# Performer and gated block on one core: the keys pass with its random features in four row tiles, one job order per engine, and the value parts kept twice

## The reference, cut to what matters

```python
q = jnp.einsum('bsd,dhk->bhsk', x, wq)
k = jnp.einsum('bsd,dhk->bhsk', x, wk)
v = jnp.einsum('bsd,dhk->bhsk', x, wv)

def _phi(u, omega):                       # omega: 128 x 32
    proj = jnp.einsum('bhsk,mk->bhsm', u, omega)
    sq = 0.5 * jnp.sum(u * u, axis=-1, keepdims=True)
    stab = jnp.max(proj, axis=-1, keepdims=True)
    return jnp.exp(proj - sq - stab) / jnp.sqrt(m) + 1e-06

pk = _phi(k * scale, omega)
kv = jnp.einsum('bhsm,bhsk->bhmk', pk, v)  # sum over the rows s
z = jnp.sum(pk, axis=2)
```

## Time and profile before

| | |
|---|---|
| median of three runs | 3862.85 us (3861.43 to 3863.89) |
| the profiled execution, its own time | 3863.65 us |
| its span, first to last instruction | 3861.9 us |
| mean granted clock of PE | 0.973 of full |
| keys pass | from 0 to about 1019 us of the span |
| groups in the keys pass | 32, one each 30.9 us in the middle |

### The profile page before, as it was taken

One profiled execution on the slowest core, in us unless ns is written; L12 is line 12 of the kernel. 1 busy time (PEld: TensorE's weight loads), 2 busy tenths in 40 slices (PEclk: granted clock), 3 DMA queues, 4 the chain that ended last, 5 costly groups with the idle time before them and its releaser, 6 DMA issues. The chain is left out here.

```text
span 3861.9 us, 70764 instructions
## 1 busy us (share of the span) xinstructions
PE 3656.8 (95%) x25330; PEld 3166.0 (82%) x25330; DVE 2275.3 (59%) x3627; ACT 1838.2 (48%) x3947; POOL 1379.4 (36%) x956
## 2 busy tenths in 40 slices
PE   7999999999599999999999976999999999999998
PEld 6777777777488888888888866888888998888987
DVE  6777777777567877878778853333333333333332
ACT  5666666666455655656556643332323323223322
POOL 3344444434334544445445441222222222222222
PEclk9999999999799999999999998999999999999999
DMA  3222222122223232223222323111111111111111
GB/s 107 85 79 75 85 81 81 71 87 82 101 83 100 85 100 92 92 85 100 87 92 91 105 79 123 44 49 50 53 43 43 43 43 43 43 43 43 43 43 49
DMA packets 155048, 282.63 MB, mean 73 GB/s; under 512 B 23568, under 2 KB 44560, under 8 KB 153872
## 3 DMA queue, kind: packets, MB, share of 16 engines
q1 hardware_dynamic: 154896, 280.42, 21.5%
HBM read 166.08 MB, written 114.29 MB: 73 GB/s over the span
## 5 line engine op out<-in xcount | busy, mean ns | idle before, releaser
L1480 DVE TENSOR_TENSOR ffn_hT_lo<-ffn_hid,ffn_hT_hi 128x512 fp32r<-128x512 f32 x256 | 334.6, 1336 | 491.0 <-ACT ffn_hT_hi L1456 491.0
L96 PE MATMUL ffn_hidden<-ffn_yT_hi,ffn_wa_hi 128*128 128x256 f32 x2048 | 573.7, 280 | 11.6 <-DVE ffn_yT_lo L1476 11.6
L96 PE MATMUL ffn_hidden<-ffn_yT_hi,ffn_wa_lo 128*128 128x256 f32 x2048 | 573.9, 280 | 0.0
L96 PE MATMUL ffn_hidden<-ffn_yT_lo,ffn_wa_hi 128*128 128x256 f32 x2048 | 572.9, 280 | 0.0
L1447 ACT ACTIVATE ffn_hid<-ffn_hidden,ffn_bias 128x256 f32<-128x256 f32 x512 | 213.2, 467 | 674.0 <-PE ffn_hidden L96 621.9
L96 PE MATMUL ffn_result<-ffn_wb_hi,ffn_hT_hi 128*128 128x512 f32 x1024 | 412.2, 403 | 7.5 <-DVE ffn_hT_lo L1480 7.4
L274 POOL TENSOR_TENSOR ffn_n_rstd<-ffn_n_base,ffn_n_power 128x2 f32<-128x2 f32 x32 | 22.4, 699 | 1080.3 <-DVE ffn_n_negmean L269 1080.3
L96 PE MATMUL ffn_result<-ffn_wb_hi,ffn_hT_lo 128*128 128x512 f32 x1024 | 404.5, 395 | 0.0
L96 PE MATMUL ffn_result<-ffn_wb_lo,ffn_hT_hi 128*128 128x512 f32 x1024 | 404.2, 395 | 0.0
L96 PEld LDWEIGHTS ffn_hidden<-ffn_yT_hi,ffn_wa_hi 128*128 128x128 f32 x2048 | 385.1, 188 | 20.6 <-DVE ffn_yT_lo L1476 11.9
L96 PEld LDWEIGHTS ffn_hidden<-ffn_yT_lo,ffn_wa_hi 128*128 128x128 f32 x2048 | 385.5, 188 | 8.9
(11 more groups left out here) (231 smaller groups left out, 10062.4 us busy)
## 6 DMA issues: line engine op xcount, KB each, us to landing
attend_uq<-u_d SPq DMA_DIRECT2D x33, 512.0 KB, 3.6
ffn_y_in<-y_d SPq DMA_DIRECT2D x33, 512.0 KB, 3.6
keys_xin<-in_L_attn_x_dram SPq DMA_DIRECT2D x32, 512.0 KB, 4.0
xn_d<-keys_xn SPq DMA_DIRECT2D x32, 512.0 KB, 2.8
xT_d<-keys_xT_whole SPq DMA_DIRECT2D x32, 512.0 KB, 2.9
u_d<-keys_uq SPq DMA_DIRECT2D x32, 512.0 KB, 2.8
attend_xTf<-xT_d SPq DMA_DIRECT2D x32, 512.0 KB, 5.0
r_d<-attend_gate SPq DMA_DIRECT2D x32, 512.0 KB, 2.8
```

Source lines behind the costliest of these rows:

```text
L96: last = pe.matmul(out, stationary[a], moving[b], start=start and n == 0, stop=stop and n == len(TERMS) - 1)
L1480: dve.tensor_tensor(hT[n % HB].lo[:, :, :], hid[n % 2][:, :, :], f32(hT[n % HB].hi[:, :, :]), ALU.subtract).then_inc(h_ready[n % HB], 1)
```

## The change

- **Features of a whole tile in four row tiles.** The matrix `bd` goes, and omega transposed (`omT`, 128 partitions that hold it four times below each other, 128 columns) takes its place. The job `proj` n is now for tile n with all its 16 heads: for each of four chunks and three terms, four matmuls, one for each head of the chunk, with 32 partitions (a row tile) by 128 columns, each into its own bank `feat[j]`. The four banks hold a whole tile, once. The second tile waits until the exponentials of the first have read them. `top` is then four reductions of 512 columns for a tile and one `below` of 16 columns. The eight banks are now two `dense`, four `feat`, one `turn` and one `kv`; before they were two each of `dense`, `turn`, `proj` and `kv`.
- **An order of jobs for each engine.** `BODY` becomes `PE_BODY`, `DVE_BODY`, `ACT_BODY`, `POOL_BODY` and `SP_BODY`. exp, hi, pk and z are jobs for one tile and one chunk (n = 4 t + c).
- **Buffers.** `v_parts` is kept twice, by the parity of the group. `e` and `pk` hold all four chunks of each tile. `kv_sum` has the whole bank, diagonal blocks and the rest, so that DVE adds 128 partitions by 512 in one operation for each chunk; the store picks the blocks that are wanted, in two DMAs. The stages for the weights lie in `e` and `z_sum`.
- **Loops.** The four groups of a sequence are written out, with a loop over sequences only.

```diff
-        BODY = [("whole", 0, 1), ("x", 0, 2), ("proj", 0, 0), ("top", 0, 0), ("hi", 0, 0), ("k", 0, 1),
-                ("top", 1, 0), ("pk", 0, 0), ("proj", 1, 0), ("hi", 1, 0), ("k", 1, 1), ("proj", 2, 0),
-                ("top", 2, 0), ("hi", 2, 0), ("pk", 1, 0), ("kv", 0, 0), ("stats", 0, 2), ("top", 3, 0), ("q", 0, 1),
-                ("norm", 0, 2), ("pk", 2, 0), ("kv", 1, 0), ("proj", 3, 0), ("hi", 3, 0), ("q", 1, 1), ("pk", 3, 0),
-                ("turn_k", 0, 1), ("turn_k", 1, 1), ("v", 0, 1), ("kv", 2, 0), ("kv", 3, 0), ("v_out", 0, 1),
-                ("v", 1, 1), ("v_out", 1, 1), ("turn_x", 0, 2), ("turn_x", 1, 2)]
+        PE_BODY = [("proj", 0, 0), ("k", 0, 1), ("k", 1, 1), ("q", 0, 1), ("proj", 1, 0), ("turn_k", 0, 1),
+                   ("q", 1, 1), ("v", 0, 1), ("turn_k", 1, 1), ("kv", 0, 0), ("v", 1, 1), ("kv", 1, 0), ("kv", 2, 0),
+                   ("turn_x", 0, 2), ("kv", 3, 0), ("turn_x", 1, 2)]
+        DVE_BODY = [("top", 0, 0), ("sq", 0, 1), ("pk", 0, 0), ("top", 1, 0), ("pk", 1, 0), ("turn_k", 0, 1),
+                    ("pk", 2, 0), ("pk", 3, 0), ("pk", 4, 0), ("stats", 0, 2), ("pk", 5, 0), ("kv", 0, 0),
+                    ("turn_k", 1, 1), ("pk", 6, 0), ("kv", 1, 0), ("pk", 7, 0), ("sq", 1, 1), ("kv", 2, 0),
+                    ("turn_x", 0, 2), ("v_out", 0, 1), ("kv", 3, 0), ("turn_x", 1, 2), ("v_out", 1, 1)]
+        ACT_BODY = [("k", 0, 1), ("exp", 0, 0), ("exp", 1, 0), ("exp", 2, 0), ("exp", 3, 0), ("hi", 0, 0),
+                    ("k", 1, 1), ("hi", 1, 0), ("q", 0, 1), ("hi", 2, 0), ("turn_k", 0, 1), ("hi", 3, 0),
+                    ("exp", 4, 0), ("hi", 4, 0), ("exp", 5, 0), ("q", 1, 1), ("hi", 5, 0), ("exp", 6, 0),
+                    ("turn_k", 1, 1), ("hi", 6, 0), ("exp", 7, 0), ("hi", 7, 0), ("norm", 0, 2), ("turn_x", 0, 2),
+                    ("v_out", 0, 1), ("turn_x", 1, 2), ("v_out", 1, 1)]
+        POOL_BODY = [("z", 0, 0), ("z", 1, 0), ("z", 2, 0), ("z", 3, 0), ("stats", 0, 2), ("z", 4, 0),
+                     ("whole", 0, 1), ("z", 5, 0), ("z", 6, 0), ("z", 7, 0)]
+        SP_BODY = [("x", 0, 2), ("whole", 0, 1), ("q", 1, 1), ("norm", 0, 2), ("sums", 0, 0)]
...
 # PE
                 if job == "proj":
-                    pe.wait_ge(turn[n // 2].free, 2 * g + 2)
-                    for t in range(TG):
-                        wait(pe, e_ready[t], NC * g + n)
-                        product(pe, proj[t].t[:, :], kT[:, n, t * P:(t + 1) * P], bd[:, :], start=True, stop=True)\
-                            .then_inc(proj[t].full, 1)
+                    pe.wait_ge(turn.free, 4 * g + 4)
+                    wait(pe, e_ready[1 - n], NC * g + NC if n == 1 else NC * g)
+                    for c in range(NC):
+                        for k, (x_, y_) in enumerate(TERMS):
+                            for j in range(HC):
+                                last = pe.matmul(feat[j].t[:, c * M:(c + 1) * M],
+                                                 kT[rows(j), c, n * P:(n + 1) * P][x_], omT[rows(j), :][y_],
+                                                 start=k == 0, stop=k == 2)
+                                if c == NC - 1 and k == 2:
+                                    last.then_inc(feat[j].full, 1)
                 if job == "kv":
-                    wait(pe, kv[n % 2].free, 2 * g + n // 2)
+                    wait(pe, kv.free, NC * g + n)
...
 # ACT
                 if job == "turn_x":
                     wait(act, xT_whole_ready, g)
-                    act.wait_ge(turn[n].full, 2 * g + 1)
+                    act.wait_ge(turn.full, 4 * g + n + 1)
...
                 if job == "v_out":
                     act.wait_ge(dense[n].full, 3 * g + 3)
-                    for m in range(2):
-                        wait(act, kv[m].full, 2 * g)
-                    act.activation(v_part[:, n, :, 0, :], by_head(dense[n].t), ACT.Copy).then_inc(v_hi, 1)
+                    wait(act, kv.full, NC * (g - 1))
+                    act.activation(v_part[i % 2][:, n, :, 0, :], by_head(dense[n].t), ACT.Copy).then_inc(v_hi, 1)
...
+                if job == "exp":
+                    t, c = n // NC, n % NC
+                    if c == 0:
+                        act.wait_ge(below_ready, TG * g + t + 1)
...
+                    wait(act, pk_ready[t], NC * (g - 1) + c + 1)
+                    wait(act, z_added[t], NC * (g - 1) + c + 1)
+                    for j in range(HC):
+                        h = c * HC + j
+                        last = act.activation(e[t][:, c, j * M:(j + 1) * M], feat[j].t[:, c * M:(c + 1) * M],
+                                              ACT.Exp, bias=below[:, t, h:h + 1])
+                    last.then_inc(e_ready[t], 1)
...
 # DVE
+                if job == "top":
+                    t = TG * g + n
+                    for j in range(HC):
+                        dve.wait_ge(feat[j].full, t + 1)
+                        dve.tensor_reduce(top[:, n, :, j:j + 1], feat[j].t[:, :].rearrange("p (c m) -> p c m", c=NC),
+                                          AX.X, ALU.max).then_inc(top_ready, 1)
+                    dve.wait_ge(sq_ready[n], g + 1)
+                    dve.wait_ge(top_ready, HC * t + HC)
+                    dve.scalar_tensor_tensor(out=below[:, n, :], in0=sq[:, n, :], scalar=-0.5,
+                                             in1=top[:, n, :, :].rearrange("p c j -> p (c j)"),
+                                             op0=ALU.mult, op1=ALU.subtract).then_inc(below_ready, 1)
...
+                    if i == 0:
+                        dve.tensor_copy(kv_sum[:, n, :], kv.t[:, :]).then_inc(kv.free, 1)
+                    else:
+                        dve.tensor_tensor(kv_sum[:, n, :], kv.t[:, :], kv_sum[:, n, :], ALU.add).then_inc(kv.free, 1)
...
 # SP
+                if job == "sums":
+                    wait_alone(sp, z_added[1], NC * g + NC, sp_passed)
+                    wait_alone(sp, kv.free, NC * g + NC, sp_passed)
+                    sp.dma_start(z_d[b], z_sum[:, :, :]).then_inc(sums_stored, 16)
+                    own = kv_sum[:, :, :].rearrange("p n (q a m) -> p (n q) a m", q=2, a=2)
+                    for a in range(2):
+                        half = slice(a * 2 * KD, (a + 1) * 2 * KD)
+                        sp.dma_start(kv_d[b][half, :, :], own[half, :, a, :]).then_inc(sums_stored, 16)
```

More of the change, by code:

```diff
@@ L191, in split_weights @@
     return load, turn, hi, lo, done, through
[L194 to L233, removed]
 class Norm:
@@ L372, in keys_pass @@
[L372 to L380, removed]
-            for job, n, g in HEAD:
[L382 to L386, removed]
-            with eng.Fori(1, n_batches - 1) as b:
[L388 to L391, removed]
-            last = n_batches - 1
-            body(last * GB, last, first=True)
-            with eng.Fori(1, GB - 2) as i:
-                body(i + last * GB, last)
-            body(G - 2, last, ahead=1)
-            body(G - 1, last, ahead=0)
-            batch_end(last)
+                ("stats", 0, 1), ("sq", 0, 0), ("q", 0, 0), ("norm", 0, 1), ("sq", 1, 0), ("q", 1, 0),
@@ new lines, in keys_pass, with run, body @@
+                ("turn_k", 0, 0), ("turn_k", 1, 0), ("v", 0, 0), ("v_out", 0, 0), ("v", 1, 0), ("v_out", 1, 0),
+                ("turn_x", 0, 1), ("turn_x", 1, 1)]
+        def run(eng, do, order):
+            def body(g, b, i):
+                for job, n, lead in order:
+                    if isinstance(g, int) and g + lead >= G:
+                        continue
+                    if job == "sums" and i != GB - 1:
+                        continue
+                    do(job, n, g + lead, b, (i + lead) % GB)
+            for job, n, g in HEAD:
+                do(job, n, g, 0, g)
+            for i in range(GB):
+                body(i, 0, i)
+            with eng.Fori(1, n_batches - 1) as b:
+                for i in range(GB):
+                    body(b * GB + i, b, i)
+            for i in range(GB):
+                body((n_batches - 1) * GB + i, n_batches - 1, i)
@@ L475, in do @@
                     act.wait_ge(norm.ready, g + 1)
-                    for m in range(2):
-                        wait(act, turn[m].full, 2 * g - 1)
+                    wait(act, turn.full, 4 * g - 2)
                     wait(act, xn_stored, 16 * g)
@@ L493, in do @@
                     act.wait_ge(dense[n].full, 3 * g + 1)
-                    for m in range(2):
-                        wait(act, turn[m].full, 2 * g)
+                    wait(act, turn.full, 4 * g)
                     wait(act, sq_ready[n], g)
@@ L508, in do @@
-                    act.wait_ge(turn[n].full, 2 * g + 2)
-                    act.activation(kT.hi[:, 2 * n:2 * n + 2, :], halves(turn[n]), ACT.Copy).then_inc(kT_hi, 1)
-                if job == "proj":
-                    for t in range(TG):
-                        act.wait_ge(below_ready[t], NC * g + n + 1)
-                        wait(act, pk_ready[t], NC * g + n)
-                        wait(act, z_added[t], NC * g + n)
```

(4 more changed lines are left out.)

195 lines of the change are left out of this document (88 added, 107 removed).

## The result

The changed kernel takes 3798.32 us (median of four runs, 3791.62 to 3801.29) against 3862.14 us of the kernel before on the same chip (3860.81 to 3863.89). The ratio is 0.9832, interval 0.9815 to 0.9849: 64 us less, where I forecast 90. That lies in the range, but the sum behind it was wrong by more than the total shows. The profiled execution took 3801.29 us, 62.4 less than that of before. By the first instruction of the next pass the keys pass ends at 983.80 instead of 1025.92 us: only 42.1 of the 62.4 are there, where the forecast put all of its 89.9. The other 20.3 came in the attend pass (1312.2 to 1299.0) and the feed forward pass (1523.8 to 1516.7), whose code is the same.

A forecast was written before the change was run, and what follows sets the result against it. PE, 95% busy, was taken to bound the old kernel; afterwards job order, with DVE late, gives 28.0 us a group. Savings of 82.5, 1.9, 4.5 and 1 make 89.9 us, hence 3773 us, range 3700 to 3840.

The forecast's parts named there:

- the sum: Keys pass savings: 82.5 us from 30 groups, 1.9 last but one, 4.5 last, 1 omega; together 89.9.
- The walk: Middle group of the keys pass, job lists followed in order: DVE late from 14.0, about 28.0 us a group; chance 0.50.
- The rival that they would not: Feature matmuls of the keys pass: row tiles do not overlap, 0.1 us each, 9.5 us a group, 3887; chance 0.02.
- `pk` beside POOL: Late in a group, DVE's `pk` 6 and 7 wait behind POOL's `z` 4 and `whole`: 1.1 and 1.8 us charged.
- charged 0.5: End of a group: hand from PE to ACT to DVE of `turn_x` 1, whose bank is single, 0.5 us.
- Value parts twice: Second `v_parts` takes away a wait of ACT that lay beside PE's work; costed at nothing.
- The failed step: Loops of the keys pass: writing out four groups adds no instruction to a group; costed at nothing.
- the price of the row tiles: Feature job on PE: 48 row-tile matmuls take 1.49 us, as in attend; two jobs 3.0 in place of 5.6.
- The head: Start of the keys pass: omega split by one operation on ACT and DVE in place of four, 1 us gained.
- The tail: Last two bodies of the keys pass: 25.5 in place of 27.4 us, and 22.8 in place of 27.3.
- the pace of the exponentials: Last body, second tile: four times exp and hi, 4 x 1.55 us.
- The slow rival: PE clock falls to 1.2 GHz ahead of `kv` 3 in each group: 31.8 us a group, 3887; chance 0.09.

The follow-up runs named there:

- small-`z` run: The changed kernel with POOL's z sums cut from 512 to 4 columns (z then wrong), whole-group sum left in place: 3801.81 us, one execution.
- run with `whole` first: The changed kernel with POOL's sum over the whole group moved to the front of its list: 3765.42 us, ratio to before 0.9765.

## Why the prediction was right in the group and wrong in the sum

- **The walk held.** From 538.31 on, after against forecast: proj 1.56 (1.5), first exponential 5.57 (5.4), `proj` 1 at 11.5 (11.3), `below` done at 14.2 (14.0), the group 27.9 (28.0). DVE is the late one, as the `kv_sum` waits show; PE idles where I said.
- **Row tiles.** They overlap: undone, a group is 7.3 longer. The rival that they would not is gone.
- **`pk` beside POOL.** Right in place, too large in size and wrong as two charges: 0.84 and 1.05 measured for 1.1 and 1.8. The small-`z` run shows that taking one away feeds the other, the run with `whole` first that moving the long one is worth 0.7. Most of the other 0.9 of DVE's time are waits for PE and ACT: 0.45 ahead of the second `kv` add (row 561.03), 0.20 ahead of the fourth, 0.29 ahead of the last split, for which I had charged 0.5; and its list starts 0.2 late.
- **Value parts twice.** I said what wait they take away, and that without them `v_out` would queue ahead of `turn_x` 1. That is what came; it is worth 0.8 us a group.
- **The failed step** is "The written-out loops add no instruction to a group". True, but the jump back over four written-out groups cost 29.8 us in five places. Taken out it goes, put into the kernel before it comes, with short bodies it is gone. What it is made of is open; the packets of the instruction queues point to the reading in of the program. The evidence lay in the trace of before: the attend pass has the written-out form, and its waits in before, from 1026 to 2338 us, read

```profile
PE attend_feat L1176 <- issue: 16.7, 9, 3.9
```

  By POOL's first `attend_mix_lo` of each group a plain group there takes 35 to 36 us, the first of a sequence that no jump leads to 44.8, and the five behind a jump 50.4 to 51.7, 5.6 to 6.9 more. I took the price of the row tiles from that pass, and not what its loop costs.
- **The head** was priced for omega alone. That gain came: the first transposes of x start at 10.82 instead of 12.13 in before. But two turn banks became one, and HEAD was left in its old order. At all three pairs of turns PE stands still, 1.50, 2.08 and 1.66, which is 5.2 of the 6.1 that the first body is late; then come 3.4 at half clock. The reordered head gives 6.5 of the 9.5 back.
- **The tail** was mis-sized by 12.0. In the last body but one `stats` is gone, so four `pk` move up beside `z` 4 and `whole` and take 6.82 for about 2.5 (row 931.44), and PE waits 2.68 for one. In the last body the first tile took 8.8 for my 8.6; the second, up to the first `kv`, 9.2 for some 7.2, its features at half clock; and the four `kv` with one bank follow each other at 967.73 - 964.90 = 2.8 us each, where I had only the pace of the exponentials, 1.55. Besides, my terms for the last body add up to some 22.1, not 22.8. This is read from the trace; no run took it apart.
- **The clock.** The slow rival fell: middle groups read 1.00, PE's idle times in them being about 1 us each. The clock did fall elsewhere, behind the stand-stills at the jumps, in the head and in the tail, as the earlier trace rows had it for the last group of before.
- **20.3 us that I did not forecast** came from passes whose code is the same, 13.2 in attend and 7.1 in feed forward. Of attend's, 10.3 lie at its own five jumps back: by the starts of POOL's first `attend_mix_lo` of each group, the steps over them are 51.4, 50.5, 50.9, 50.4 and 51.7 in before and 50.2, 48.8, 50.0, 48.7 and 47.0 after, and the other steps are the same to within 0.9 in all. Over all kernels here the two passes together run from 2805.5 (`whole` first) to 2836.0 (before), with no edit in them. Each of these is one execution; those of one kernel differ by up to 16 us, so differences among the later kernels (2805.5 to 2820.5) may be no more than that. That a jump costs another amount when the same code lies elsewhere in the program is a guess, and where the 7.1 come from is open. That the forecast lies in its range is partly luck: this made up for two fifths of what the sum had wrong in the keys pass.

## What to carry to other kernels

Writing a loop body out four times is not free even when it adds no instruction: look for "issue" waits just behind a loop's jump, in this pass or a sister that already has the form, and price them per jump. Compare what the instruction queues move around a cheap and a costly jump. Walk the steady group, but walk the head and the tail with the same lists and banks too: a bank given up is paid where its jobs stand next to each other. On engines that get in each other's way, move the long operation beside operations that it does not hold up (here, those of DVE with at most one input in SBUF), rather than trimming the short ones.

## What the runs showed of the hardware

- A jump back over four written-out groups cost 5 to 9 us in most cases, 0.1 to 0.9 in some, and 10.5 to 11.5 in the run with features over all rows. Nineteen jumps over one or two written-out groups cost nothing that can be seen. Around the costly jumps the instruction queues moved packets; around the cheap ones q8 moved none.
- Four 32-row by 128-column matmuls in row tiles, each in its own bank, take 0.11 us together, four over 128 rows 0.45.
- Beside a POOL operation, a DVE operation on 128x512 with both inputs in SBUF took 1.16 us in the median and up to 2.03 us instead of 0.68; those with at most one input there took 0.67 to 0.69 either way.
- Passes that no edit touched took up to 30 us less in one kernel's profiled execution than in another's, and 10.3 of the attend pass's 13.2 between before and after lie at its jumps. A change in a sister pass is to be read from its own stretch, not from the total.
